# Layer norm's factor and offset moved from the weights into ScalarE's copies, and the weight splits into other steps

## The reference

```python
xn = _layernorm(x)                      # no factor, no offset
s  = causal attention of xn: q, k, v = xn @ w.T, rotated, softmax(q k / 16) v   # one head of 256
for l in range(2):                      # the layer, on y, which begins as xn
    h = shift_token(y)                  # second half of the columns moved one row down
    q, k, v = split(h @ wqkv[l])        # 8 heads of 64, l2-normed, scaled, rotated
    y = y + local_attention(q, k, v) @ wo[l]      # window of 128
    h = shift_token(y)
    h = (h - mu) / sqrt(var + 1e-05) * lg[l] + lb[l]
    a, g = split(h @ w1[l] + b1[l])     # 2 x 682 hidden
    y = y + (a * gelu(g)) @ w2[l] + b2[l]
out = x + s * silu(y)
```

## Time and profile before

| | us |
|---|---|
| median of 3 runs | 1464.69 (1464.49 to 1465.24) |
| the profiled execution's own time | 1466.16 |
| its span, first to last instruction | 1464.4 |
| busy: PE | 1397.7 (95%) |
| busy: VectorE (DVE) | 961.4 (66%) |
| busy: ScalarE (ACT) | 853.1 (58%) |
| busy: GpSimd (POOL) | 754.2 (52%) |
| mean granted TensorE clock | 0.983 |

### The profile page before, as it was taken

One profiled execution on the slowest core, in us unless ns is written; L12 is line 12 of the kernel. 1 busy time (PEld: TensorE's weight loads), 2 busy tenths in 40 slices (PEclk: granted clock), 3 DMA queues, 4 the chain that ended last, 5 costly groups with the idle time before them and its releaser, 6 DMA issues.

```text
span 1464.4 us, 24262 instructions
## 1 busy us (share of the span) xinstructions
PE 1397.7 (95%) x7828; PEld 1066.0 (73%) x7828; DVE 961.4 (66%) x2664; ACT 853.1 (58%) x2175; POOL 754.2 (52%) x514
## 2 busy tenths in 40 slices
PE   5999978999999999999999999999999999999987
PEld 5778766677777777777776767777777777777766
DVE  5767657666666666667576767676766666666666
ACT  3555555564646465656566574747474747565763
POOL 2333336383837373737474643747373738383810
PEclk9999989999999999999999999999999999999998
DMA  7111020000000000000001010000000000000037
GB/s 213 30 57 52 20 68 1 1 1 1 0 0 0 0 0 0 0 0 0 0 1 46 14 59 1 1 0 0 0 0 0 0 0 0 0 0 0 0 106 238
DMA packets 35239, 33.28 MB, mean 23 GB/s; under 512 B 8364, under 2 KB 32896, under 8 KB 35200
## 3 DMA queue, kind: packets, MB, share of 16 engines
q1 hardware_dynamic: 35200, 32.79, 7.0%
HBM read 24.39 MB, written 8.39 MB: 22 GB/s over the span
## 4 chain that ended last, share of the span: by engine, by line
PE 72%; ACT 6%; issue 3%; DVE 1%; POOL 1%; DMA 1%; ACTq 0%; SPq 0%; DVEq 0%; POOLq 0%
PE l_psF L1271 9%; PE l_ring L1245 9%; PE l_psP L1245 9%; PE l_ring L1271 7%; PE l_ring L1340 7%; PE l_psP L1324 7%; PE l_psF L1358 6%; PE l_psS L1281 5%; ACT l_att L943 4%; PE l_psS L1293 4%; PE l_psF L1310 4%; PE l_ring L1281 2%; PE l_psS L1310 2%; PE l_psF L1252 1%; PE l_psF L1256 1%
## 5 line engine op out<-in xcount | busy, mean ns | idle before, releaser
L812 POOL TENSOR_TENSOR l_att<-l_att 128x1024 f32<-128x1024 f32 x64 | 154.1, 2408 | 322.6 <-DVE l_att L1054 322.6
L859 POOL TENSOR_TENSOR l_att<-l_att,l_rinv 128x1024 f32<-128x1024 f32 x64 | 121.2, 1894 | 66.9 <-DVE l_rinv L1111 66.0
L923 ACT ACTIVATE l_att<-l_psP 128x384 f32<-128x384 f32 (+1 forms) x128 | 70.2, 548 | 130.5 <-PE l_psP L1324 130.5
L828 POOL TENSOR_TENSOR l_u_lo<-l_att,l_u_hi 128x512 fp32r<-128x512 f32 x90 | 115.4, 1291 | 58.2 <-ACT l_u_hi L918 58.2
L1116 DVE COPY l_att<-l_psP 128x384 f32<-128x384 f32 (+1 forms) x128 | 78.8, 616 | 85.5 <-PE l_psP L1324 85.2
L1324 PE MATMUL l_psP<-ident,l_att 128*128 128x128 f32 x896 | 125.2, 280 | 2.2 <-DVE l_att L1116 1.5
L1324 PEld LDWEIGHTS l_psP<-ident,l_att 128*128 128x128 f32 x896 | 99.2, 142 | 32.1 <-issue 30.0
L819 POOL TENSOR_TENSOR l_att<-l_att,l_rn 128x1024 f32<-128x1024 f32 x64 | 121.6, 1913 | 0.0
L943 ACT ACTIVATE l_att<-l_psF,l_nb 128x256 f32<-128x256 f32 x256 | 117.8, 483 | 0.0
L1104 DVE CUSTOM_DVE_ANT_0 l_psF<-l_psF,w_mask 128x256 f32<-128x256 f32 x256 | 101.0, 455 | 24.2 <-issue 24.2
L1340 PE MATMUL l_ring<-l_att 128*64 128x256 f32 (+1 forms) x1024 | 111.5, 360 | 1.4 <-ACT l_att L923 1.4
(11 more groups left out here) (203 smaller groups left out, 4064.3 us busy)
## 6 DMA issues: line engine op xcount, KB each, us to landing
a_tables<-in_x SPq DMA_DIRECT2D x8, 512.0 KB, 4.2
scratch_s<-a_o SPq DMA_DIRECT2D x8, 512.0 KB, 3.0
l_att<-in_x SPq DMA_DIRECT2D x8, 512.0 KB, 8.7
l_att<-scratch_s SPq DMA_DIRECT2D x8, 512.0 KB, 9.7
out_dram<-l_att SPq DMA_DIRECT2D x7, 512.0 KB, 6.3
aw_stage<-in_wqkv SPq DMA_DIRECT2D x2, 768.0 KB, 7.5
l_att<-in_wqkv SPq DMA_DIRECT2D x2, 768.0 KB, 5.2
w_w_raw<-in_w SPq DMA_DIRECT2D x2, 640.0 KB
```

The source lines that it names most:

```text
L812: pool.tensor_tensor(rot[:, t, :], rot[:, t, :], t2[t % 2], ALU.add).then_inc(S["added"], 1)
L828: pool.tensor_tensor(U_lo[0:rows, j, :], gate_of(j, attn)[0:rows, :], U_hi[0:rows, j, :].bitcast(F32), ALU.subtract).then_inc(S["u_lo"], 1)
L859: pool.tensor_tensor(pr, pr, along(inv, 2 * P), ALU.mult).then_inc(S["p_done"], 1)
```

## The change

1. Norm. `lg` and `lb` are no longer folded into the weights. `b1_products`, `b1_columns` and the scale in the split of `w1` go. In every FFN half ACT now makes `fhi` with two instructions (one per half of the columns) that multiply and add with a value per partition, and then `affine()`, two more instructions of the same kind, writes the product in place over `dF`, for the low part. The low part (POOL, in step 16 DVE) waits for `affine_done`. `hidden(0)` waits for `fhi` alone, does its 8 matmuls of `fhi`, then waits for `flo` and does the other 4.
2. Weights of layer 0. `w1` gets a staging buffer of its own and is loaded at the start. Step 6 of the attention block is taken out of the loop. Steps 6, 7 and 8 carry the splits: `wqkv` in three parts by columns in step 6, `w1` and `wo` in step 7, `w2` in step 8. The low parts of `wo` and `w2` are made by POOL, the tables (L329) by POOL at the end of step 6. PE waits for each part where it is used.
3. The turn. The split of `wqkv` at the end of step 7 is in three parts by columns, and PE starts after the first. `wo` is split in the softmax's units 4 (ACT) and 5 (DVE), the low part of `w1` after the last low part of o, that of `w2` after h of step 8 is made, which is before the rotation of step 9.
4. Step 0 of the layers: DVE adds and scales the last of the four tiles (`finish`) in place of POOL.

The diff, cut to what these four do:

```diff
     def high_w1(self, act, layer, stage, k):
         act.wait_ge(self.S["w1_in"], 64 * (layer + 1))
-        act.wait_ge(self.S["small"], self.SMALL)
-        act.activation(self.w1_hi[:, k, :], stage[:, k, :], ACT.Copy, scale=self.gcol[:, layer, k:k + 1]).then_inc(self.S["w1_hi"], 1)
+        act.activation(self.w1_hi[:, k, :], stage[:, k, :], ACT.Copy).then_inc(self.S["w1_hi"], 1)
...
+    def low_wqkv(self, dve, layer, stage, c):
+        dve.wait_ge(self.S["wq_hi"], 3 * layer + c + 1)
+        cols = slice(c * INNER, (c + 1) * INNER)
+        dve.tensor_tensor(self.wq_lo[:, :, cols], stage[:, :, cols], self.wq_hi[:, :, cols].bitcast(F32), ALU.subtract).then_inc(self.S["wq_lo"], 1)
...
-    def b1_products(self, pe, layer, stage, ps):
...
-                last = pe.matmul(ps[:, j:j + 1], stage[:, k, j * P:(j + 1) * P], self.bcol[:, layer, k:k + 1], start=(k == 0), stop=(k == KD - 1))
...
-        stage1 = tables[:, 0:KD * W1T * P].rearrange("p (k n) -> p k n", k=KD)
+        stage1 = sb("aw_stage1", [P, KD, W1T * P])
...
                 W.load_wo(sp, 0)
+                sp.wait_ge(S["w_tr"], 3)
+                W.load_wqkv(sp, 0, stage_q)
+                W.load_w1(sp, 0, stage1)
                 sp.wait_ge(WS["w2pad"], 1)
                 W.load_w2(sp, 0)
...
                         pool.tensor_tensor(dst[:, :, :, 1], src[:, :, :, 0], tab[:, :, :, 1], ALU.mult).then_inc(S["t2_done"], 1)
-                else:
+                if isinstance(i, int) and i == B - 2:
                     layer_tables()
+                if isinstance(i, int) and i == B - 1:
+                    W.low_wo(pool, 0)
+                if isinstance(i, int) and i == B:
+                    W.low_w2(pool, 0)
...
+                if front:
+                    rotate(i, 2)
+                    rotate(i, 3)
+                if isinstance(i, int) and i == B - 2:
+                    for c in range(3):
+                        W.low_wqkv(dve, 0, stage_q, c)
+                if isinstance(i, int) and i == B - 1:
                     for k in range(KD):
                         W.low_w1(dve, 0, stage1, k)
...
                 def low_f():
-                    ge(pool, S["f_hi"], i)
+                    ge(pool, S["affine_done"], i)
...
                 def high_f():
                     ge(act, S["hn_done"], i)
-                    act.activation(fhi[:, :, :], dF, ACT.Copy).then_inc(S["f_hi"], 1)
+                    for k in range(KD):
+                        last = act.activation(fhi[:, k, :], dF[:, k], ACT.Identity, scale=W.gcol[:, lf, k:k + 1], bias=W.bcol[:, lf, k:k + 1])
+                    last.then_inc(S["f_hi"], 1)
+
+                def affine():
+                    for k in range(KD):
+                        last = act.activation(dF[:, k], dF[:, k], ACT.Identity, scale=W.gcol[:, lf, k:k + 1], bias=W.bcol[:, lf, k:k + 1])
+                    last.then_inc(S["affine_done"], 1)
...
                 if ffn:
                     high_f()
+                    affine()
                 if attn:
                     evacuate(i, 3)
...
+            def finish(i, t):
+
+                n = TT * i + t + 1
+                ge(dve, S["added"], n - 1)
+                ge(dve, S["turned"], 2 * n)
+                dve.tensor_tensor(rot[:, t, :], rot[:, t, :], t2[t % 2], ALU.add).then_inc(S["added"], 1)
+                ge(dve, S["rn_done"], n)
+                ge(dve, S["added"], n)
+                ge(dve, S["rot_done"], n - 1)
+                r = heads_of(rot[:, t, :], 2 * HEADS)
+                dve.tensor_tensor(r, r, along(rn[:, t, :], DH), ALU.mult).then_inc(S["rot_done"], 1)
...
                     rotate(i, 3, la)
+                if not ffn:
+                    finish(i, TT - 1)
                 for j in range(HT):
...
+                if turn:
                     for k in range(KD):
-                        W.low_wqkv(dve, 1, stage, k)
-                if turn:
-                    W.low_w2(dve, 1)
+                        W.low_w1(dve, 1, stage1, k)
                 if attn:
                     ge(dve, S["wo_ps"], i + 1)
...
+                if turn:
+                    W.low_w2(dve, 1)
             pipeline(dve, step)
...
             def hidden(i, j, attn):
                 u = i - 1
-                ge(pe, S["f_lo"], i)
+                ge(pe, S["f_hi"], i)
...
+                terms = [(k, w, fhi) for k in range(KD) for w in (w1_hi, w1_lo)] + [(k, w1_hi, flo) for k in range(KD)]
...
+                for wanted in (("hi", "lo") if j == 0 else ("hi lo",)):
+                    if wanted != "hi":
+                        ge(pe, S["f_lo"], i)
...
-                        if turn and u == UNITS + 1:
-                            W.b1_products(pe, 1, stage1, psS[:, N:2 * N])
```

More of the change, by code:

```diff
@@ L409, in step @@
                     norm(i + 1)
[L410 to L411 removed]
+                prepare(i, 0)
                 if back:
@@ L425, in step @@
                     out(i, 3)
-                if not front:
-                    for k in range(KD):
-                        W.high_w1(act, 0, stage1, k)
-                    W.high_wo(act, 0)
-                    W.high_w2(act, 0)
                 if front:
@@ L665, in step @@
                     values(i, 3)
-                if not front:
-                    W.b1_products(pe, 0, stage1, psT)
                 if front:
@@ L1384, in step @@
                     return
-                if turn:
-                    pe.wait_ge(WS["wq_lo"], KD * LAYERS)
                 if attn:
-                    project(i, 0)
+                    project(i, 0, la if turn or not ffn else None)
                 if attn and ffn:
```

126 lines of the change are left out of this document (54 added, 72 removed).

## The result

| | before | changed |
|---|---|---|
| median of the runs, us | 1464.84 (1463.94 to 1466.42) | 1471.38 (1469.65 to 1472.48) |
| ratio to before, 95% interval | | 1.0042 (1.0032 to 1.0052) |
| profiled execution, span | 1464.4 | 1467.7 |
| busy PE, DVE, ACT, POOL | 1397.7, 961.4, 853.1, 754.2 | 1386.4, 966.3, 878.0, 757.7 |

What follows compares the result with a forecast made beforehand. The prediction took PE, busy for 95% of the span, as the bound. Its terms 7.2 - 9.9 + 0.1 + 0.8 + 1.8 summed to 0.0, giving 1464.7 us; range 1457 to 1471, the forecast's own 1461.5 to 1468.

Steps and rivals of the forecast that it cites:

- A: Steady steps: four ScalarE instructions instead of one delay the k copy and PE's transposes(1), +0.55 per step, +7.2 us.
- B: The turn, steps 7 to 9: no b1 products, moved weight splits; together -9.9 us (-11.5 to -8).
- C: Attention block: splits and tables take turns, the end no longer waits for b1 products; sum +0.1 us (-4 to +3).
- D: Step 0: VectorE's addition and scaling stand before the k copies PE's transposes need, +0.8 us (-0.5 to +1.3).
- E: Step 16: the added instructions count in full, with nothing beside the last FFN, +1.8 us.
- Rival 4: Steady steps: POOL becomes the bound, passes 1.4 longer, 0.6 per step on top, +7.8, 1472.5 us; chance 0.15.
- F: Loads at the start: w1 ahead of batch 2's x on SP's queue costs 0, at most 0.5 us.

Runs made afterwards that it cites:

- again: The changed kernel itself run a second time, no edit: 1470.96 us, ratio 1.0039 to the kernel before.
- plain_copies: The changed kernel with its four new ScalarE instructions as plain copies, without the norm's factor and offset: 1461.35 us, ratio 0.9979.
- k_copy_first_in_before: The kernel before, with VectorE making the k copy of j = 0 before gated(0): 1464.60 us, ratio 0.9998.
- square_between: The changed kernel with ScalarE's order high_f, tile 3's q square, affine, its k square, then tile 2's inverse norm: 1467.38 us, ratio 1.0015.
- norm_alone: The kernel before with only the norm part of the change; weight splits, step 0 and turn as before: 1469.45 us, ratio 1.0027.

## Why the prediction was right and wrong

The measured time lies at the upper end of the range, 1471 (1471.38, and 1470.96 in again), so it is 3.4 us above the forecast's own range, and "no change that can be measured" was wrong. Between the profiles, on which the sum was made, the span is 3.3 us longer where the sum said 0.0: A is 1.2 too low, B 0.7, C 1.0 and D 1.35, and E is 1.1 too high. No single rival came true. Rival 4's number, 1472.5, is the nearest, but POOL's passes held nothing in the steady step of the change.

- **A** (+7.2): 13 x 0.64 = +8.4. Right in mechanism, place and wait: the square, VectorE's rotation, the k copy, `transposes(1)`. Both sizes were a little off, with the same sign. The instruction starts 0.705 us after the last, not 0.68, and the slack of 0.16, taken as a middle of 0 and 0.32, is none (plain_copies, k_copy_first_in_before). Part of it was luck: by these two alone the step should be about 0.8 longer (an estimate: the square 1.87 us later, with 1.09 to spare before VectorE's rotation in the kernel before), but `high_f` starts 14.81 us after the step's first matmul, where it was 14.99, since PE's `project` is faster (last section); this gave some 0.2 back. That `low_f` and POOL's passes cost nothing was right in the change, and no further: a half microsecond later `flo` holds PE (square_between). The row of 0.90 us against 0.87 said that there was no slack; the middle of two bounds was a worse estimate than that row.
- **B** (-9.9): the turn -9.9, step 7 -1.1 beside its A, step 9 +1.8: -9.2. Right. The wait for VectorE's `w2` came as foreseen, 0.3 larger.
- **C** (+0.1): +1.1, in again +1.7. That the splits and the tables take turns was right, and their end at 173.16 right to a tenth of a microsecond; this was partly luck, as the splits took 6.71 and not the 3.3 + 3.78 of the sum, and began 0.4 later. Two things were missed: the scores after the wait ran in part at the low clock, 0.9 us (0.2 in again), and the end of step 7 cost more (the last values are 5.6 us later in all, where the sum had 4.1). The -4.8 at the end came out as -4.5, though not for the reason given: the earlier trace rows were read as a wait for PE alone, and VectorE ended later than PE, as norm_alone shows.
- **D** (+0.8, at most +1.3): **the step that failed.** It was +2.15 in the profile, outside its bounds; with part 4 undone step 0 is 62.9, with it 65.8 to 68.3, so 2.9 to 5.4 us, of which 2.2 stand with the time at the low clock equal. The term priced the addition at 1.2; it met POOL's scaling and took 2.03, by the very rule that C had used. And the wait was put on PE at its length alone, without the clock behind it.
- **E** (+1.8): +0.7 in the profile, +0.9 in again, +2.3 in norm_alone, against 49.7 before. The four instructions count in the chain as said: from the start of `high_f` to PE's first transposes behind it it is 1.69 us before (1428.12 to 1429.81), 3.56 in the change (1430.54 to 1434.10) and 3.55 in norm_alone. What differs is `hidden(0)` behind them, in the chain of waits 4.44 us before, 3.52 in the change and 4.37 in norm_alone: PE was idle before it and runs the first of its matmuls at the low clock, fewer in the change. The term left that out.
- **F** (0): the attention block's step 7 begins at the same time as before (the second mask of its scores at 171.10 against 171.20; 171.75 in again).

The difference of the medians, 6.5, is larger than the 3.3 of the profiles: the profiled execution of the change was 1.7 us below its median, with the shortest step 0 of all profiles with part 4, and that of the kernel before 1.3 above its own.

## What to carry to other kernels

When an engine is busy without a pause ahead of a wait of the critical one, every tenth put before it counts in every repetition; look in the two queues for an instruction that stands behind another without needing it, as the k copy did. A gap in VectorE's timeline is not free for a difference or product of two SBUF tiles if POOL has one there too: here the two took turns (6.71 us in place of 3.49), and moving one of them moved the collision (5.30 in place of 3.15), until it stood where nothing waited. Price a new wait of TensorE with the clock behind it, by a row in which the same form ran after such a wait.

## What was not expected of the hardware

PE's `project` became faster by itself. The second and third kind of its matmuls (128x512) have medians of 388 and 392 ns in the changed kernel, 396 and 395 before, and 12 take 2.76 us in place of 2.80, with the same code and the granted clock at 1.00 in both:

```profile
L1245 PE MATMUL l_ring<-w_wq_lo,l_hhi x192: 392/396/628, 217.3 to 1355.1; 128*128 128x512 f32 x192
```

```profile
L1259 PE MATMUL l_ring<-w_wq_lo,l_hhi x192: 387/388/628, 218.5 to 1356.9; 128*128 128x512 f32 x192
```

It is so in every kernel with part 1, norm_alone too, and in neither of the two that keep the b1 products. That the addresses of the buffers moved with the removed one is a guess that no run tried. Little of it shows in the time, since VectorE or `flo` sets the step: only where the chain leaves PE late in `project`, as in the change, does ScalarE start earlier by it, some 0.2 us per step by the two timelines.

The other is that two profiles of the same program differ by 3.5 us in the time that TensorE spends at its low clock in one step (6.8 and 10.3 us of the same 20).
